# Three float32r passes over split operands in place of one plain float32 matmul in the channel mix

## What is computed

```
y = einsum('bct,bcd->bdt', x, cond_weights[condition])
z = einsum('bsd,od->bso', y, W) + b
u = einsum('bsd,edr->ebsr', y, A)
m = einsum('ebsr,ero,e->bso', u, B, p_scores)
gamma = min(0.5 * norm(z) / (norm(m) + 1e-6), 1)      # norms over the last axis
out = x + z + gamma * m
```

## Time and profile before

| | us |
|---|---|
| median of 3 runs | 1031.05 (1029.73 to 1031.88) |
| the profiled execution, first to last instruction | 1029.6 |
| TensorE, matmuls busy | 1017.3 (99%) |
| TensorE, weight loads busy | 856.4 (83%) |
| VectorE busy | 351.2 (34%) |
| ScalarE busy | 289.2 (28%) |
| GpSimd busy | 165.2 (16%) |

### The profile page before, as it was taken

One profiled execution on the slowest core, in us unless ns is written; L12 is line 12 of the kernel. 1 busy time (PEld: TensorE's weight loads), 2 busy tenths in 40 slices (PEclk: granted clock), 3 DMA queues, 4 the chain that ended last, 5 costly groups with the idle time before them and its releaser, 6 DMA issues.

```text
span 1029.6 us, 15207 instructions
## 1 busy us (share of the span) xinstructions
PE 1017.3 (99%) x5260; PEld 856.4 (83%) x5260; DVE 351.2 (34%) x620; ACT 289.2 (28%) x685; POOL 165.2 (16%) x263
## 2 busy tenths in 40 slices
PE   7999999999999999999999999999999999999997
PEld 5888888888888888888888888888888888888885
DVE  4433233233333332332333333323323333233332
ACT  5322223223223322232232232222322322222211
POOL 0211111111111111111111111111111111111112
PEclk9999999999999999999999999999999999999999
DMA  8112122121221211211212212112112122121111
GB/s 324 52 74 79 44 81 75 48 81 41 81 81 41 81 66 57 81 61 61 81 41 81 81 41 81 61 62 81 57 65 81 41 81 81 41 81 49 74 42 41
DMA packets 21367, 73.58 MB, mean 71 GB/s; under 512 B 2409, under 2 KB 3434, under 8 KB 21354
## 3 DMA queue, kind: packets, MB, share of 16 engines
q1 hardware_dynamic: 21354, 73.41, 19.6%
HBM read 39.85 MB, written 33.55 MB: 71 GB/s over the span
## 4 chain that ended last, share of the span: by engine, by line
PE 98%; DMA 1%; DVE 0%; ACT 0%; SPq 0%; issue 0%; DVEq 0%; POOLq 0%; POOL 0%; ACTq 0%
PE z_ps L439 70%; PE mix_ps L419 11%; PE m_ps L456 9%; PE u_ps L430 9%; DMA x_in<-in_x_dram 1%; DVE w_lo L327 0%; SPq L172 0%; ACT w_hi L241 0%; DVE rows L408 0%; DVE rows L368 0%; DVEq L59 0%; ACT squares L289 0%; POOLq L59 0%; ACT y_hi L245 0%; SPq L170 0%
## 5 line engine op out<-in xcount | busy, mean ns | idle before, releaser
L439 PE MATMUL z_ps<-w_hi,y_hi 128*128 128x512 f32 x1024 | 415.9, 406 | 2.2 <-DVE w_lo L327 2.2
L439 PE MATMUL z_ps<-w_hi,y_lo 128*128 128x512 f32 x1024 | 405.8, 396 | 0.0
L439 PE MATMUL z_ps<-w_lo,y_hi 128*128 128x512 f32 x1024 | 405.4, 396 | 0.0
L289 ACT ACTIVATE squares<-rows 128x512 bf16<-128x512 f32 x128 | 80.8, 631 | 628.2 <-DVE rows L368 536.8
L439 PEld LDWEIGHTS z_ps<-w_hi,y_lo 128*128 128x128 f32 x1024 | 192.7, 188 | 46.3
L439 PEld LDWEIGHTS z_ps<-w_hi,y_hi 128*128 128x128 f32 x1024 | 193.4, 189 | 43.0 <-ACT y_hi L245 2.4
L439 PEld LDWEIGHTS z_ps<-w_lo,y_hi 128*128 128x128 f32 x1024 | 193.4, 189 | 40.9
L368 DVE TENSOR_TENSOR rows<-z_ps,bias 128x512 f32<-128x512 f32 x128 | 88.6, 692 | 365.7 <-PE z_ps L439 365.7
L333 DVE TENSOR_TENSOR y_lo<-mix_ps,y_hi 128x512 fp32r<-128x512 f32 x128 | 88.2, 689 | 232.7 <-ACT y_hi L245 232.5
L224 POOL TENSOR_TENSOR rows<-rows,x_in 128x512 f32<-128x512 f32 x64 | 81.7, 1277 | 428.0 <-DVE rows L368 428.0
L419 PEld LDWEIGHTS mix_ps<-mixer,x_in 128*128 128x128 f32 x1024 | 131.3, 191 | 10.8 <-DMA x_in<-in_x_dram 2.3
(11 more groups left out here) (38 smaller groups left out, 479.8 us busy)
## 6 DMA issues: line engine op xcount, KB each, us to landing
x_in<-in_x_dram SPq DMA_DIRECT2D x64, 512.0 KB, 3.3
out_dram<-rows SPq DMA_DIRECT2D x63, 512.0 KB, 2.7
rows<-in_L_ffn_W_dram SPq DMA_DIRECT2D x4, 512.0 KB, 7.4
w_late<-in_L_ffn_W_dram SPq DMA_DIRECT2D x4, 512.0 KB, 11.0
cond_all<-in_L_cond_weights_dram SPq DMA_DIRECT2D x2, 256.0 KB, 4.0
a_in<-in_L_ffn_A_dram SPq DMA_DIRECT2D x1, 512.0 KB, 14.3
bm_in<-in_L_ffn_B_dram SPq DMA_DIRECT2D x1, 512.0 KB, 8.9
bias<-in_L_ffn_b_dram SPq DMA_DIRECT2D x1, 512.0 KB, 9.2
```

Of the source, the lines that this page charges most:

```text
L289: nc.scalar.activation(squares[:, cols], z_b[:, j % 2, cols], ACT.Square, accum_out=z_sq[:, j % 2, h:h + 1]).then_inc(z_squared, 1)
L439: summed = nc.tensor.matmul(z_ps[h][:, :], left[:, g, k, r], right[:, k, h * H:(h + 1) * H], start=(k == 0 and n == 0), stop=(k == KC - 1 ...
```

## The change

The mix gets split operands too. ScalarE casts the whole of `cond_all` once into the hi part of `cond_hl` and VectorE makes the lo part; `make_mixer` copies both parts of a sample's matrix in one instruction into a `mixer` with two parts. A new `split_x` on ScalarE casts a tile of x to `x_hi` (128 by 1024), a new `split_x` on VectorE makes `x_lo`. `mix` issues three matmuls where it issued one. TensorE waits for `x_lo_ready` where it waited for `x_loaded`. In the step of tile t, ScalarE's `split_x(j+3)` stands behind `make_mixer(t+3)` and ahead of the squares of m, VectorE's stands behind `split_y(j+2, 1)`. The core of the diff:

```diff
-        mixer = sb("mixer", [P, 2, P], fp32)
+        cond_hl = sb("cond_hl", [P, E, 2, C], fp32r)
+        mixer = sb("mixer", [P, 2, 2, P], fp32r)
+        x_hi = sb("x_hi", [P, 2, D], fp32r)
+        x_lo = sb("x_lo", [P, 2, D], fp32r)
...
 (ScalarE)
+            def split_x(j, loads, mixed):
+                act.wait_ge(x_loaded[j % BODY], loads)
+                if mixed is not None:
+                    act.wait_ge(mix_done, mixed)
+                nc.scalar.copy(x_hi[:, j % 2, :], x_in[:, j % BODY, :]).then_inc(x_hi_ready, 1)
...
-                    made = nc.scalar.copy(mixer[part, j % 2, q * C:(q + 1) * C],
-                                          cond_all[part, bass.ds(e, 1), :].rearrange("p e d -> p (e d)"))
+                    made = nc.scalar.copy(mixer[part, j % 2, :, q * C:(q + 1) * C],
+                                          cond_hl[part, bass.ds(e, 1), :, :].rearrange("p e s d -> p (e s) d"))
...
+            nc.scalar.copy(cond_hl[:, :, 0, :], cond_all[:, :, :]).then_inc(cond_hi_ready, 1)
+            split_x(0, 16, None)
+            act.wait_ge(cond_hi_ready, 1)
+            act.wait_ge(cond_lo_ready, 1)
             act.wait_ge(mixer_zeroed, 1)
             for t in range(2):
                 make_mixer(t, t)
...
                     if not opening and (not last or j + 3 < BODY):
                         act.wait_ge(mix_done, 2 * t + 4)
                         make_mixer(t + 3, j + 3)
+                        split_x(j + 3, 16 * (i + (j + 3) // BODY + 1), 2 * t + 4)
                     act.wait_ge(m_done, t + 1)
...
 (VectorE)
+            def split_x(j, t):
+                dve.wait_ge(x_hi_ready, t + 1)
+                nc.vector.tensor_tensor(x_lo[:, j % 2, :], x_in[:, j % BODY, :], x_hi[:, j % 2, :].bitcast(fp32),
+                                        ALU.subtract).then_inc(x_lo_ready, 1)
...
                     if not last or j + 2 < BODY:
                         dve.wait_ge(y_hi_ready, 2 * t + 6)
                         split_y(j + 2, 1)
+                    if not opening and (not last or j + 3 < BODY):
+                        split_x(j + 3, t + 3)
...
 (TensorE, mix)
-                    mixed = nc.tensor.matmul(mix_ps[h][:, k * P:(k + 1) * P],
-                                             x_in[:, j % BODY, (h * HC + k) * P:(h * HC + k + 1) * P],
-                                             mixer[:, j % 2, :], start=True, stop=True)
+                    c = slice((h * HC + k) * P, (h * HC + k + 1) * P)
+                    passes = [(x_hi, 0), (x_hi, 1), (x_lo, 0)]
+                    for n, (left, part) in enumerate(passes):
+                        mixed = nc.tensor.matmul(mix_ps[h][:, k * P:(k + 1) * P], left[:, j % 2, c],
+                                                 mixer[:, j % 2, part, :], start=(n == 0), stop=(n == 2))
...
-                        pe.wait_ge(x_loaded[(j + 2) % BODY], 16 * (i + (j + 2) // BODY + 1))
+                        pe.wait_ge(x_lo_ready, t + 3)
```

More of the change, by code:

```diff
@@ L135, in conditioned_clamped_low_rank_linear_kernel @@
         b_lo_ready = sem("b_lo_ready")
+        cond_hi_ready = sem("cond_hi_ready")
+        cond_lo_ready = sem("cond_lo_ready")
         mixer_ready = sem("mixer_ready")
+        x_hi_ready = sem("x_hi_ready")
+        x_lo_ready = sem("x_lo_ready")
         mix_done = sem("mix_done")
@@ L212, in _ @@
             nc.gpsimd.memset(half[:, :], 0.5).then_inc(half_set, 1)
-            nc.gpsimd.memset(mixer[:, :, :], 0.0).then_inc(mixer_zeroed, 1)
+            nc.gpsimd.memset(mixer[:, :, :, :].bitcast(fp32), 0.0).then_inc(mixer_zeroed, 1)
             pool.wait_ge(half_set, 1)
@@ L271, in _ @@
                     make_mixer(2, 2)
+                if k == MIX_1_AFTER - 1:
+                    split_x(1, 16, None)
                 if k >= KC - 2:
@@ L274, in _ @@
                     split_y(1, k - KC + 2)
+            split_x(2, 16, 2)
             act.wait_ge(a_loaded, 16)
@@ L296, in step @@
                         make_mixer(3, 3)
+                        split_x(3, 16, 4)
                     if j % 2 == 0:
@@ L334, in split_y @@
                                         y_hi[part].bitcast(fp32), ALU.subtract).then_inc(y_lo_ready, 1)
+            dve.wait_ge(cond_hi_ready, 1)
+            nc.vector.tensor_tensor(cond_hl[:, :, 1, :], cond_all[:, :, :], cond_hl[:, :, 0, :].bitcast(fp32),
+                                    ALU.subtract).then_inc(cond_lo_ready, 1)
+            split_x(0, 0)
             for k in range(KC):
@@ L340, in _ @@
                 split_w(k)
+                if k == MIX_1_AFTER - 1:
+                    split_x(1, 1)
                 if k >= KC - 2:
@@ L343, in _ @@
                     split_y(1, k - KC + 2)
+            split_x(2, 2)
             dve.wait_ge(a_hi_ready, 1)
@@ L374, in step @@
                         split_y(2, 0)
+                        split_x(3, 3)
                     if j % 2 == 0:
@@ L461, in _ @@
                 nc.tensor.matmul(u_ps[:, :], idle[:, 0:P], idle[:, :], start=True, stop=True)
-            pe.wait_ge(x_loaded[0], 16)
+            pe.wait_ge(x_lo_ready, 1)
             pe.wait_ge(mixer_ready, 1)
@@ L478, in _ @@
                 if k == MIX_1_AFTER:
-                    pe.wait_ge(x_loaded[1], 16)
+                    pe.wait_ge(x_lo_ready, 2)
                     pe.wait_ge(mixer_ready, 2)
@@ L482, in _ @@
                         mix(1, h)
-            pe.wait_ge(x_loaded[2], 16)
+            pe.wait_ge(x_lo_ready, 3)
             pe.wait_ge(mixer_ready, 3)
```

## The result

The changed kernel takes 1092.8 us (median of 4 runs, 1092.1 to 1093.1) against 1031.1 of before: a ratio of 1.060 (95% interval 1.058 to 1.061), 61.6 us slower. The forecast was 1091.6. The profiled execution spans 1090.6 us against 1029.6.

What follows compares the result with a forecast made beforehand. TensorE, busy 99% of the span, was taken to bound the kernel. 55.2 us for 124 mix halves plus 5.4 for the start gave +60.6 us: 1090.2 profiled, 1091.6 as median; range 1045 to 1124.

Steps and rivals of the forecast that it cites:

- The term of the loop: Mix on TensorE: 8 pairs of load and matmul become 12 at 0.111 us; +0.445 us a half, 55.2 us over 124 halves.
- the hidden load: Mix on TensorE: consecutive float32r loads overlap, a half costs 0.70 us, the kernel gets faster, about 1013 us; chance 0.06.
- the partial overlap: Mix on TensorE: loads overlap in part, a pair takes 0.08 us, a half 0.96 us, time 1045 us; chance 0.04.
- the third: Mix on TensorE: narrow float32r runs as slowly as a plain product, 0.222 us each, time 1262 us; chance 0.08.
- The rule of passes: Mix on TensorE: true FP32 takes four array passes, so three stand for four and a half falls to 0.67 us.
- The other engines: ScalarE and VectorE in the loop: new casts and subtractions cost 0; x_lo is in time with 0.8 us to spare.
- The start: Before the loop: mix starts 2.5 us later, first half at the lower clock, W's splits later; +5.4 us, left 3 to 9.
- the step on how the splits of W pace what follows: Start, ScalarE and VectorE: W's parts come one after another with tile 1's split between; chunk 4 at about 24.0, before 19.6.
- Behind it nothing waits: After the start: TensorE's own queue is longer than that of the splits, so no further wait arises.

## Why the prediction was right

**The term of the loop.** The step was: a float32r load of 128 by 128 takes 0.11 us and at 128 moving columns nothing covers it, so 8 pairs become 12 and a half grows by 0.445 us. Measured: 0.11 us a pair and 0.452 us for a half, 124 x 0.452 = 56.0 us where 55.2 was forecast. The evidence used was the lone load of the earlier trace rows; the run with 64 moving columns shows that the load sets the step and the run with 64 stationary columns that it would go with the load. Of the rivals the hidden load (1013) and the partial overlap (1045) had the right rate for the columns, 0.06 us, but not for this load; the third (1262) asked for 0.222 us a pair where 0.112 was measured, and is answered by the run with 64 stationary columns as well.

**The rule of passes.** Three passes for four was the reckoning that asked for a gain. It fell short because TensorE here is paid by the pair of load and matmul, of which the plain product has two and not four. The Trainium skill's count of four passes ("FP8 and Floating Point Precision", section TensorE Precision Notes) is no price here: the trace shows two pairs of 0.111 us for a plain product. What the array does within one of them no run here shows.

**The other engines.** The rows of the changed kernel, ScalarE and VectorE in order of time, in a step of the tight kind:

```profile
534.49 1.05 ACT L260 CAST x_hi<-x_in 128x1024 fp32r<-128x1024 f32 x1
535.44 1.02 ACT L336 ACTIVATE squares<-m_ps 128x1024 bf16<-128x1024 f32 x1
...
537.66 1.22 DVE L356 TENSOR_TENSOR x_lo<-x_in,x_hi 128x1024 fp32r<-128x1024 f32 x1
...
539.89 0.33 PE L461 MATMUL mix_ps<-mixer,x_hi 128*128 128x128 f32 x2
```

`x_lo` is there at 538.9, TensorE's mix comes at 539.9: 1.0 us to spare where 0.8 was worked out. No wait on `x_lo` stands in the loop.

**The start.** Forecast +5.4 us in all. The first `up` in the chain before the change; then the first matmul of the mix after it and the chain of the start after, to be held against the earlier trace rows; last the one wait that was not foreseen:

```profile
31.75 1.63 PE m_ps L456 x6
...
10.17 0.66 PE L461 MATMUL mix_ps<-mixer,x_hi 128*128 128x128 f32 x2 [3.88 <-ACT mixer L267]
...
10.17 2.81 PE mix_ps L461 x12
...
16.06 7.39 PE z_ps L480 x24
23.47 1.63 PE z_ps L480 x6
25.11 1.30 PE mix_ps L461 x12
...
38.02 1.64 PE m_ps L497 x6
...
PE m_ps L497 <- DVE u_lo L414: 0.6, 1, 0.6
```

The mix began at 10.2 (forecast 10.5), the first half ran at the lower clock (2.8 us, forecast 2.7), the first linear matmul came at 16.1 (16.1). In part this was luck: in this execution the cast of x began at 6.93, so x had landed a microsecond earlier than forecast, and the copies into the mixer came last and not `x_lo`; in the execution with 28 matmuls on zeros x landed at 8.27 and `x_lo` came last. Chunk 4 started at 23.5, and 24.0 was forecast, so the step on how the splits of W pace what follows was 0.5 us too high. "Behind it nothing waits" was wrong by about as much: in the step of tile 0 VectorE makes `x_lo` of tile 3 ahead of `u_lo`, and the first `up` waited 0.6 us for that. The two errors cancel: the first `up` came at 38.02 instead of 31.75, 6.3 us later, of which 0.9 are the two halves of the mix of tile 2, and 5.4 are left for the start. So the sum is 56.0 + 5.4 = 61.4 us where 60.6 was forecast; measured are 61.0 between the profiled executions and 61.6 between the medians. What little is missing from the forecast is the 0.445 for 0.452 us of a half, 0.8 us in all.

## What to carry to other kernels

Price a matmul as a pair. In these runs it cost the longer of its columns' streaming and its weight load, and with a float32r stationary block of 128 columns the load needs 0.11 us. By that, fewer than about 240 moving columns (an estimate: 0.11 us by 0.456 ns for one) buy nothing. To trade a plain float32 matmul for three float32r passes, count pairs, 2 against 3: at 128 moving columns it loses. No run here has a plain float32 matmul with more moving columns, so whether the trade pays there is open. If a narrow product has to be split, split it into a type with a short load, and see that the extra splits are not queued ahead of what the start is waiting for.

## What the runs showed of the hardware

A plain float32 matmul is recorded as two weight loads and two matmuls (8 for 4 products, 0.111 us a pair), a float32r or bfloat16 one as one of each. A second pass over the same stationary block is loaded again: the two `x_hi` passes show a load each (1024 for 512 products). The size of the gap between types was not expected: a pair of 128 by 128 with 128 moving columns takes 0.11 us in float32r and 0.057 us in bfloat16, as little as float32r with half the stationary columns (0.06). And 64 moving columns in place of 128 changed nothing, neither the time (1092.7 and 1092.8) nor the mean matmul record (268 and 270 ns). The lower clock costs less than twice: at a granted clock of 0.50 (10.2 to 15.2 us and 16 to 19 us of the changed kernel) a pair of the mix took 0.213 us (loads of `x_lo` from 10.52 to 11.16, three pairs on) where it takes 0.112 at 1.00, and a linear matmul 0.43 us (16.62 to 17.05) where it takes 0.233.
